# Streaming matmuls amid the small matmuls of two expert stages, and in the waits of a windowed attention

## The reference

```
x = x + L0_conv(ln(x));  t = t + L0_ffn(ln(t))    # selective scan; recurrence over 1024 tokens
x = x + L1_conv(ln(x));  t = t + L1_ffn(ln(t))    # 3x3 convolution; experts
x = x + L2_conv(ln(x));  t = t + L2_ffn(ln(t))    # equivariant layer; recurrence over 1024 tokens
x = x + L3_conv(ln(x));  t = t + L3_ffn(ln(t))    # windowed attention; experts
```

```
probs = softmax(x @ gate_w.T + gate_b, over tokens);  vals, idx = top_k(probs, 8)
pooled = sum_k x[idx] * vals                      # one vector for each image and expert
out = gelu([pooled, 1] @ weight1) -> [h, 1] @ weight2
outputs[idx] += out * vals
```

## Time and profile before

| | us |
|---|---|
| runs | 972.47, 974.67, 975.45; median 974.67 |
| profiled execution | 975.6, span 973.8 |
| TensorE busy | 889.0 (91%) |
| VectorE busy | 414.4 (43%) |
| ScalarE busy | 446.7 (46%) |
| GpSimd busy | 239.2 (25%) |
| mean granted TensorE clock | 0.974 |

### The profile page before, as it was taken

How to read it: one execution, slowest core, us unless ns; L and a number is a source line. 1 busy time by engine, 2 the same in 40 slices (tenths; PEclk the granted TensorE clock), 3 DMA queues, 4 the chain that set the end, 5 groups by cost and what they waited for, 6 DMA issues and landing times. The chain is left out here.

```text
span 973.8 us, 15415 instructions
## 1 busy us (share of the span) xinstructions
PE 889.0 (91%) x6191; PEld 518.6 (53%) x6272; DVE 414.4 (43%) x714; ACT 446.7 (46%) x1498; POOL 239.2 (25%) x144
## 2 busy tenths in 40 slices
PE   8778889888989888899999999999999999999887
PEld 5336667767845444344444444455555544554543
DVE  5699999999966753500000000002005400202763
ACT  5777777776636531333333333333333333334641
POOL 4149999998910000300000000000000000000410
PEclk9989999999999996999999999999999999999987
DMA  3110000000000000200000000000000000000000
GB/s 82 23 43 2 1 1 1 1 1 1 1 7 1 1 25 11 83 1 1 1 1 1 1 1 1 1 1 1 1 1 1 1 1 1 1 1 2 1 25 11
DMA packets 10220, 8.30 MB, mean 9 GB/s; under 512 B 7246, under 2 KB 8510, under 8 KB 10052
## 3 DMA queue, kind: packets, MB, share of 16 engines
q1 hardware_dynamic: 10148, 7.31, 3.1%
HBM read 5.47 MB, written 0.26 MB: 6 GB/s over the span
## 5 line engine op out<-in xcount | busy, mean ns | idle before, releaser
L908 PE MATMUL L2p_z<-stream 128*128 128x512 bf16 x880 | 342.2, 390 | 0.0
L950 ACT ACTIVATE L2yx<-L2p_z 32x2 f32<-32x2 f32 x1024 | 165.3, 161 | 323.0 <-PE L2p_z L927 323.0
L927 PEld LDWEIGHTS L2p_z<-L2yx,L2v 64*32 64x32 f32 x2048 | 137.6, 104 | 224.7 <-ACT L2yx L950 218.5
L927 PE MATMUL L2p_z<-L2yx,L2v 64*32 64x2 f32 x2048 | 225.5, 178 | 16.9 <-ACT L2yx L950 15.9
L788 POOL TENSOR_TENSOR hc<-hs,cb 128x1024 f32<-128x1024 f32 x64 | 149.6, 2363 | 4.4 <-DVE hs L729 4.4
L558 PEld LDWEIGHTS p_y<-ident,hc 128*128 128x128 f32 x1024 | 123.2, 192 | 16.5 <-POOL hc L788 9.1
L1641 DVE COPY xn_one<-L2yx 32x512 f32<-32x512 f32 (+1 forms) x2 | 0.8, 384 | 302.7 <-ACT L2yx L950 302.7
L558 PE MATMUL p_y<-ident,hc 128*128 128x128 f32 x1024 | 125.4, 276 | 4.3 <-POOL hc L788 4.3
L1641 POOL COPY xn_one<-L2yx 32x128 f32<-32x128 f32 x1 | 0.3, 284 | 484.2 <-SPq L1984 484.2
L729 DVE TENSOR_TENSOR_SCAN hs<-d_a,p_bb 128x1024 f32<-128x1024 f32 x48 | 109.8, 2287 | 6.2
L908 PEld LDWEIGHTS L2p_z<-stream 128*128 128x128 bf16 x943 | 90.1, 96 | 15.1
(11 more groups left out here) (522 smaller groups left out, 898.2 us busy)
## 6 DMA issues: line engine op xcount, KB each, us to landing
y_l<-in_pick SPq DMA_DIRECT2D x1, 768.0 KB
b_parts<-part SPq DMA_DIRECT2D x6, 128.0 KB, 2.3
c_parts<-part SPq DMA_DIRECT2D x6, 128.0 KB, 2.4
pos<-in_pos SPq DMA_DIRECT2D x1, 512.0 KB, 3.6
ao<-in_at_o SPq DMA_DIRECT2D x1, 512.0 KB, 4.0
L1w<-in_L_w SPq DMA_DIRECT2D x1, 297.0 KB
L3w<-in_L_w SPq DMA_DIRECT2D x1, 297.0 KB
above<-in_x SPq DMA_DIRECT2D x2, 128.0 KB, 3.1
```

Source lines behind the costliest of these rows:

```text
L908: pe.matmul(p_z[:, 1, 0:each], stream[:, 0:128], stream[:, 0:each], start=True, stop=True)
L927: pe.matmul(p_step[:, t % 2], v[:, 0:C], yx[:, NB * t:NB * (t + 1)], start=True, stop=True).then_inc(s("preact"), 1)
L950: act.activation(yx[0:C, NB * (t + 1):NB * (t + 2)], p_step[:, t % 2], ACT.Sigmoid).then_inc(s("state"), 1)
```

## The change

In the expert stages a stream is put amid each half of the turning and behind each half (one before, behind both), one amid the first linear layer and one amid the second. In the attention four streams go ahead of `sum_squares` and two instead of one behind it; near the end five behind a new wait for `at_max`, two after the last turns of scores, two after the last value step and one after the turn of run 3.

```diff
                     for h in range(2):
                         pe.wait_ge(*at("weights", h + 1))
                         for j in range(PER):
+                            if j == PER // 2:
+                                fill(1)
                             t = (PER * h + j) * 128
                             last = pe.matmul(p_t[:, 1 - h, j * G:(j + 1) * G], wt[:, t:t + 128], shares[:], start=True, stop=True)
                         last.then_inc(s("w_turned"), 1)
-                    fill(1)
+                        fill(1)
...
                     for t in range(TRIOS):
+                        if t == TRIOS // 2:
+                            fill(1)
                         last = pe.matmul(p_t[:, 0, 6 * t:6 * t + 6], w1[:, t], pooled[:, t], start=True, stop=True)
...
                     for e in range(E):
+                        if e == E // 2:
+                            fill(1)
                         last = pe.matmul(p_e[:, 2 * e:2 * e + 2], w2[:, e], hid[:, 2 * e:2 * e + 2], start=True, stop=True)
...
                         self.centre_new(pe)
+                        keep_streaming(pe, p_o, 4)
                         self.sum_squares(pe)
-                        keep_streaming(pe, p_o, 1)
+                        keep_streaming(pe, p_o, 2)
...
                         values(20)
                         values(21)
+                        pe.wait_ge(sig["at_max"], NJ * 12)
+                        keep_streaming(pe, self.p_tok[:], 5)
                         mix_run(2)
                         turn(22)
                         turn(23)
+                        keep_streaming(pe, self.p_tok[:], 2)
                         values(22)
                         values(23)
+                        keep_streaming(pe, self.p_tok[:], 2)
                         turn_across("x1", 1)
                         turn_run(3)
+                        keep_streaming(pe, self.p_tok[:], 1)
                         mix_across1(0)
```

## The result

The changed kernel is slower: median 982.54 us over 6 runs (979.67 to 983.83) against 974.75 for the kernel before (6 runs beside them), ratio 1.0077 with a 95% interval of 1.0059 to 1.0095. The forecast, 968.1 us and faster, was wrong in sign.

A forecast was written before the change was run, and what follows sets the result against it. TensorE, busy almost throughout, was taken to lose time where its clock falls to 1.2 GHz. Gains 3.86 - 0.51 + 1.1 + 2.2 = 6.65 us gave a forecast of 968.1 us, range 965.5 to 973.3.

The forecast's parts named there:

- L1 experts: L1 expert stage and the block behind it: 5.21 us from the higher clock less 1.35 for streams, net gain 3.86.
- if the clock stays up so far: Condition on L1's 5.21 us: TensorE at 2.4 GHz through L1's experts and the next block's layer norm.
- Price of a stream: Five more streams in each expert stage, on TensorE's own path: 0.27 us each, 1.35 us a stage.
- The row used in the prediction: L1 timeline: a stream's weights load starts at 364.86, the next useful one at 365.18, so 0.32 us a stream.
- The mark set in the prediction: Forecast called wrong if a stream costs over 0.4 us at 2.4 GHz.
- L3 experts: L3 expert stage: gain 0.33 us if the clock holds, cost 1.35 if it falls; middle taken, cost 0.51.
- the 0.8 named: L3's turning, expected longer by three streams, 0.8 us, as a sign that the forecast is right.
- Start of the attention: Four streams fill the wait before 899.07, value steps run at 2.4 GHz: gain 1.1 us, with 0.1 for an overrun.
- End of the attention: Streams in the idle stretch near 933 keep 2.4 GHz, last mix at 939.7 instead of 941.88: gain 2.2 us.
- The slower rival: L1, 899.2 and 933.3 all fall as before and the streams are load: 980.2 us, chance 0.05.

The follow-up runs named there:

- experts_only: The experts' ten streams without the attention's edits, against the kernel before: +14 us by the median.
- l1_five: The kernel before with the five streams in the L1 experts alone: cost 8.8 us by the median (984.1).
- after_ten: The changed kernel with two streams instead of one in each of its ten expert-stage places: 8.2 us below the changed kernel.
- l1_ten: The kernel before with two streams in each of L1's five new places, without the attention's edits: 9.2 us below the same with one each.
- att_mid: The attention's edits without the experts', plus eight streams in two bare waits of the attention: median 974.11 us, that of before.
- att_mid_l3: The attention's edits, eight streams in two waits between them, and L3's ten streams: 0.2 us above its best-case range of 972 to 973.5.
- e2_twenty: The kernel before with 20 instead of 17 streams at the end of the equivariant block: cost 8.6 us.
- l3_five: The kernel before with the five streams in the L3 experts alone: 981.0 us, ratio 1.0065.
- attention_only: The attention's edits without the experts', against the kernel before: within 0.3%.
- ten_mid_e2: ten_mid with 20 instead of 17 streams at the end of the equivariant block: 3.4 us more than ten_mid (medians).
- ten_mid: The changed kernel with two streams in each of ten expert-stage places and eight in two attention waits: 972.33 us against 974.43 before.

## Why the prediction was wrong

**L1 experts (3.86 gained; the profile shows 2.76 lost by the spread, 1.31 by L2). This is the step that failed.** Its condition, "if the clock stays up so far", wasn't met: the clock fell at 369.1, at the pooled copies, and the 17.1 us stretch was whole. Five streams were too few: in none of the four profiles with five there (the changed kernel twice, `experts_only`, `l1_five`) did the clock reach the first layer. With ten it held through both layers in all four, to 5.2 to 16.1 us behind the pooled copies. Then the terms came out: in `after_ten`, from spread to the next block's turn 376.89 - 374.10 = 2.79 us (forecast 2.82), from spread to first add 1.10 (1.13), pooled copies to spread 5.67 with four streams in it (5.2 with two). The speeds were right, the condition was assumed. Even met, it paid little: ten streams cost 3.0 us in L3's profile, and `l1_ten` as a whole is equal to before. Nor are the streams the whole story: of eleven profiles without a new stream in L1, the fall came within 0.5 us of the pooled copies in seven, and 4.1 to 4.4 us behind them in four (`att_mid`, `att_mid_l3`, `e2_twenty`, `l3_five`), whose way from there to the spread took 4.69 to 4.97 us, about L3's time. The forecast took the place of the fall in one profile as fixed.

**Price of a stream (0.27; measured at full clock 0.43 in the turning, 0.13 amid the first layer, 0.43 amid the second).** The layers' prices are from L3: pooled copies to GELU 2.23 us against 2.10 in before, GELU to the second layer's result 1.98 against 1.55. Five streams cost 1.85 us at full clock where the forecast has 1.35, so 1.0 us more for both stages. The row used in the prediction, 0.32 from a stream's weights load to the next useful one, starts at that load and leaves out what the stream costs ahead of it; that this is the missing 0.1 is not shown. The mark set in the prediction (wrong if a stream costs over 0.4) was passed in the turning.

**L3 experts (0.51 lost; measured 2.84).** 1.30 in the turning against the 0.8 named, 0.56 by the layers, 0.5 more in the tail, where the last fall came 1.75 us ahead of the spread (966.4 and 968.15) and in before 0.1 ahead; and 0.47 net up to the logits from the norm's fall at 945.9, which no rival had here.

**Start of the attention (1.1 gained; measured 0.2 lost).** The wait's streams held the clock in `attention_only`: six value steps 0.89 us apart, 1.3 us gained. In the changed kernel the clock fell again over the four streams, which then overran by 0.4, and the value steps won back 0.24. The sum had 0.1 for an overrun; that the streams might themselves meet the fall was not in it.

**End of the attention (2.2 gained; 2.1).** Right in place and size, in the changed kernel and in both runs of the attention alone.

**What was left out.** The forecast priced each place by itself and took unedited code as fixed. The slower rival came nearest (980.2), but wanted all of L1, 899.2 and 933.3 to fall; 933.3 held, and the kernel was slower still, because what the end gained was followed by a fall in L3's norm. Of the 7.8 us between the medians the profiled executions show 4.1. The runs of the changed kernel had 57 us at 1.2 GHz in the mean, its profiled one 49: 8 x 0.4 = 3.2 us, an estimate. Where in those runs the further falls lie, no trace shows.

**What stays open.** Why 0.64 us in `e2` brings 20 us more at 1.2 GHz, and 3.4 us of loss even in `ten_mid_e2`. The profiles show the falls at another point of the work, but each is one execution. In that of `ten_mid_e2` 10 of the 12 us that it has at 1.2 GHz beyond `ten_mid`'s lie ahead of the edit in `e2` (3.4 from 65.5 and 10.2 from 376.1, less 3.4 from 198.7), so it doesn't show where the 3.4 us of the medians come from. The fall at 65 us stands ahead of every edit and goes with the start of the execution: it is in the eleven profiles in which TensorE came to full clock 5.8 to 7.5 us into the span, and in none of the nine in which it came after 4.2 to 5.4 us. So a part of the difference between any two profiles here is no effect of an edit. And four or six timed runs are few for a kernel such as before, which has 18 of 113 runs over 60 us at 1.2 GHz.

## What to carry to other kernels

Streams that are to hold the clock pay only if they hold it: look for the stretch at 0.50 in the trace of the change first, and if it is still there, try twice as many in the same places before taking them out, since the second in a place costs half of the first. Put them in waits, where they are free, ahead of places amid small matmuls, where one cost up to 0.43 us on the path. Then look for the next thin stretch in code that wasn't edited, and compare the time at 1.2 GHz of many runs: one profile, or one place, says little of the median. Where two profiles are compared, take a pair whose falls ahead of the edit lie alike.

## What was not expected of the hardware

- At 2.4 GHz a stream of 512 columns between the small float32 matmuls of the turning takes 0.43 us, amid the first linear layer 0.13, amid the second 0.43; a second one behind it adds 0.20 to 0.22.
- TensorE at 1.2 GHz costs some 0.4 us of span for each us across the runs of before (0.42 over 113), whose instructions are the same; 0.19 to 0.55 in the other kernels.
- TensorE 92% busy (3.05 of 3.30 us) with small turns, pooling and streams lost the clock at 369.1, as it had with fewer streams. With ten streams, at 12.96 of 14.10 us, no higher a share, it kept it.
- Three or six extra streams (0.64 or 1.3 us) ahead of a recurrence of some 490 us changed where the clock fell behind it; for six, a profile whose falls ahead of them agree within 0.02 us shows it.
- With the same instructions up to there, L1's stretch at 1.2 GHz was 17.1 us long in some executions and 10.2 in others, and a fall at 65 us was there or not with the time at which TensorE first came to full clock.
